# Hybrid layers on one core: the attention mask written by ScalarE, VectorE's rotary step moved between subtraction and row sums

## What is computed

```
x = x + linear_attention(layernorm(x))
x = x + ffn(layernorm(x))
x = x + retention(layernorm(x))
x = x + ffn(layernorm(x))
```

```
q, k = l2norm(q) * qs, l2norm(k) * ks           # then rotary tables with a scale
sim  = q k^T * 8, over this block of 32 keys and the one before
sim  = where(key after query, or more than 32 before it, or no such block, -max, sim)
x    = softmax(sim) v Wo + x
x    = (a * gelu(gate)) W2 + b2 + x             # a, gate = layernorm(shift(x)) W1 + b1
```

## Time and profile before

| what | value |
|---|---|
| median of three runs | 3166.11 us |
| profiled execution, its own time | 3168.24 us |
| its span | 3166.5 us |
| busy share: TensorE, VectorE, ScalarE, GpSimd | 95%, 91%, 72%, 57% |
| mean granted clock of TensorE | 0.99 of full |

### The profile page before, as it was taken

How to read it: one execution, slowest core, us unless ns; L and a number is a source line. 1 busy time by engine, 2 the same in 40 slices (tenths; PEclk the granted TensorE clock), 3 DMA queues, 4 the chain that set the end, 5 groups by cost and what they waited for, 6 DMA issues and landing times.

```text
span 3166.5 us, 93664 instructions
## 1 busy us (share of the span) xinstructions
PE 3005.7 (95%) x37896; PEld 1857.5 (59%) x37896; DVE 2880.3 (91%) x2671; ACT 2272.7 (72%) x3707; POOL 1807.9 (57%) x823
## 2 busy tenths in 40 slices
PE   8699999999999999999999999999999999999996
PEld 4356555665665566565566656556656555665653
DVE  5599999999999999999999999999999999999995
ACT  4467777777777777776667777777777777777774
POOL 8556565555656555555445565555656565555652
PEclk9799999999999999999999999999999999999998
DMA  9544544543544544454344354454445445445542
GB/s 317 169 110 116 144 115 107 145 122 98 156 117 101 144 117 117 118 154 113 84 133 106 91 152 117 107 133 124 112 121 141 112 122 133 112 118 134 125 112 59
DMA packets 254405, 398.04 MB, mean 126 GB/s; under 512 B 51148, under 2 KB 84872, under 8 KB 254280
## 3 DMA queue, kind: packets, MB, share of 16 engines
q1 hardware_dynamic: 254280, 396.41, 47.8%
HBM read 64.64 MB, written 19.92 MB: 27 GB/s over the span
## 4 chain that ended last, share of the span: by engine, by line
PE 40%; DVE 23%; ACT 19%; issue 10%; SPq 1%; POOL 1%; DMA 1%; DVEq 0%; ACTq 0%; POOLq 0%
PE ps L848 6%; PE ps L806 5%; PE ps L866 5%; PE ps L882 5%; PE ps L827 5%; PE ps L787 4%; ACT f_ab L1094 4%; DVE f_mx L1362 4%; DVE f_p L1365 3%; ACT f_u L1093 3%; DVE f_p L1377 3%; ACT ps L1105 3%; PE ps L789 3%; PE ps L788 3%; ACT f_p L1111 3%
## 5 line engine op out<-in xcount | busy, mean ns | idle before, releaser
L1291 POOL TENSOR_TENSOR f_w<-f_w,f_ab 128x1024 f32<-128x1024 f32 x192 | 549.2, 2861 | 526.9 <-DVE f_w L1342 526.9
L1296 POOL TENSOR_TENSOR f_ab<-f_w,f_rn 128x1024 f32<-128x1024 f32 x192 | 594.1, 3094 | 390.9 <-DVE f_rn L1352 380.9
L1287 POOL TENSOR_TENSOR f_u<-f_u 128x512 f32<-128x512 f32 x384 | 589.1, 1549 | 365.3 <-ACT f_u L1093 359.8
L1094 ACT ACTIVATE f_ab<-ps,f_pa 128x512 f32<-128x512 f32 x768 | 542.1, 706 | 1.2
L1093 ACT ACTIVATE f_u<-ps 128x512 f32<-128x512 f32 x768 | 467.1, 608 | 99.3 <-PE ps L789 93.6
L1342 DVE TENSOR_TENSOR f_w<-f_ab,f_tan 128x1024 f32<-128x1024 f32 x384 | 500.4, 1343 | 4.1 <-POOL f_ab L1296 2.3
L848 PEld LDWEIGHTS ps<-f_tb,f_v 128*64 128x64 f32 x6144 | 396.0, 137 | 102.1 <-issue 78.5
L848 PE MATMUL ps<-f_tb,f_v 128*64 128x160 f32 (+1 forms) x6144 | 442.2, 297 | 11.9 <-DMA f_tb<-f_pt 10.7
L1105 ACT ACTIVATE ps<-ps 128x512 f32<-128x512 f32 x384 | 204.7, 574 | 340.7 <-PE ps L806 340.2
L787 PE MATMUL ps<-f_xh,f_wh 128*128 128x512 f32 x768 | 380.7, 496 | 54.8 <-ACT f_ab L1094 44.5
L806 PE MATMUL ps<-f_u,f_ones 128*128 128x512 f32 x768 | 370.2, 604 | 6.9 <-POOL f_u L1287 4.1
(11 more groups left out here) (165 smaller groups left out, 4822.9 us busy)
## 6 DMA issues: line engine op xcount, KB each, us to landing
f_kb<-f_ab SPq DMA_DIRECT2D x384, 256.0 KB, 3.6
f_qb<-f_ab SPq DMA_DIRECT2D x384, 256.0 KB, 3.6
f_tb<-f_pt SPq DMA_DIRECT2D x1344, 64.0 KB
f_wh<-split_w SPq DMA_DIRECT2D x48, 384.0 KB, 4.4
f_wl<-split_w SPq DMA_DIRECT2D x48, 384.0 KB, 4.2
a_w_raw<-wqkv SPq DMA_DIRECT2D x24, 384.0 KB, 4.6
split_w<-a_w_hi SPq DMA_DIRECT2D x24, 384.0 KB, 4.6
split_w<-a_w_lo SPq DMA_DIRECT2D x24, 384.0 KB, 5.5
```

Source lines behind the costliest of these rows:

```text
L1094: nc.scalar.activation(ab[:, g % 2, i, :], bank("qk", g, i), ACT.Identity, scale=pa[:, g, i:i + 1]).then_inc(qk_read.sem, 1)
L1287: nc.gpsimd.tensor_tensor(u[:, 2 * i + 1, :], u[:, 2 * i, :], u[:, 2 * i + 1, :], ALU.add).then_inc(sq_sum[i].sem, 1)
L1291: nc.gpsimd.tensor_tensor(w[:, 0:2, :], w[:, 0:2, :], ab[:, k % 2, 0:2, :], ALU.add).then_inc(q_sum.sem, 1)
L1296: nc.gpsimd.tensor_tensor(ab[:, k % 2, 0:2, :], w[:, 0:2, :], rn[:, 0:1, :].broadcast_to([128, 2, N]), ALU.mult).then_inc(rope_q.sem, 1)
```

## The change

- ScalarE gets a function `mask_scores(g)`: one copy of the table, read twice, into both banks 5 and 6 (128 partitions x 1024 elements). It waits for the subtraction of the quad before. It stands in ScalarE's order after `evacuate_out(-3)` (quad -1), before `inverse_norms(1)` (quad 0), before `shifted` (quad 1) and after `next_high` (quad 2); in retention steps quad 2's stands after `gates`.
- TensorE loses both mask matmuls and the identity that they used. `scores(g)` waits for ScalarE's copy and increments a semaphore that nobody waits for. At the start of the kernel two matmuls write both banks once.
- In plain steps, `scores(0)` goes in front of the last of the four banks of `project(2)`.
- In plain steps, VectorE does `turn(1)` between `less_maximum(-1)` and `sums(-1)`, and `turn(2)` between `less_maximum(0)` and `sums(0)`; before, `turn(1)` stood after `sums(-1)`, and `turn(2)` after `residual`. Retention steps had this place for `turn(2)` already.
- Step 0 gets a wait in `norms`.

The diff, with most of the unchanged lines left out:

```diff
@@ -464,6 +464,7 @@
         s_ready = per_quad("s_ready", ahead=2)
+        m_ready = per_quad("m_ready")
         s_max, s_sub, p_exp = per_quad("s_max"), per_quad("s_sub", ahead=1), per_quad("p_exp")
@@ -480,6 +481,7 @@
         R.update(g0=Signal("r_g0"), g1=Signal("r_g1", 2), g2=Signal("r_g2"))
+        scores_begun = sem("scores_begun")
         r_consts, r_turned, stored = sem("r_consts"), sem("r_turned"), sem("stored")
@@ -489,7 +491,7 @@
                     *((128, c) for c in range(-64, 33, 32)), *((512, c) for c in range(-640, -255, 128))]
-        ACT_USES = [(1, -1), (3, -5), (3, -4), (3, -3), *((4, c) for c in range(-3, 2)), *((8, c) for c in range(-7, 1)),
+        ACT_USES = [(1, -1), (3, -5), (3, -4), (3, -3), *((4, c) for c in range(-4, 2)), *((8, c) for c in range(-7, 1)),
                     *((16, c) for c in range(-15, 1)), (32, 32), *((128, c) for c in range(-96, 1, 32))]
@@ -507,7 +509,6 @@
                 mask, ones = t("mask", [128, 768], BF16), t("ones", [128, 128])
-                identb = t("identb", [128, 128], BF16)
                 xs, xh, x1 = t("xs", [C, N]), t("xh", [C, N], F32R), t("x1", [C, N])
@@ -533,7 +534,7 @@
                 split_first = sem("f_split_first", scope)
-                N_CONST, N_MASKED = 6 * 16, 3
+                N_CONST, N_MASKED = 6 * 16, 2
                 block = scope.enter_context(nc.Block())
@@ -799,6 +800,9 @@
+        if not prev and g:
+            pe.wait_ge(gain.sem, now.count(gain, g - 1))
         for i in range(2):
@@ -806,15 +810,12 @@
-    def mask_scores(g):
-
-        pe.wait_ge(s_sub.sem, now.count(s_sub, g - 1))
-        nc.tensor.matmul(ps[:, SS[0], :], identb[:, :], mask[:, 128:640], start=True, stop=False, skip_group_check=True)
-
...
         pe.wait_ge(k_dma.sem, now.count(k_dma, g))
-        nc.tensor.matmul(ps[:, SS[1], :], identb[:, :], mask[:, 128:640], start=True, stop=False, skip_group_check=True)
+        pe.wait_ge(m_ready.sem, now.count(m_ready, g))
+        pe.sem_inc(scores_begun, 1)
         for tile in range(TILES):
@@ -952,7 +953,6 @@
         project(0, (0, 1))
-        mask_scores(-1)
         project(0, (2, 3))
@@ -966,7 +966,6 @@
         project(1, (2, 3))
-        mask_scores(0)
         project_out(0)
@@ -983,7 +982,6 @@
         mean()
-        mask_scores(1)
         project(3, (0, 1))
@@ -992,7 +990,6 @@
         ret_values()
-        mask_scores(2)
         ret_project("q")
@@ -1003,8 +1000,6 @@
-    if prev:
-        mask_scores(-1)
     if cur:
@@ -1012,6 +1007,9 @@
             pe.wait_ge(masked, N_MASKED)
+            for i in range(2):
+                nc.tensor.matmul(ps[:, SS[i], :], ones[:, :], tan2[:, 0, :], start=True, stop=True).then_inc(masked, 1)
     if prev:
@@ -1029,15 +1027,13 @@
         norms(1)
-        mask_scores(0)
-        project(2, range(4))
+        project(2, range(3))
         scores(0)
+        project(2, (3,))
         project_v(1, range(2))
...
         values(-1)
-    if cur:
-        mask_scores(1)
     if prev:
@@ -1106,6 +1101,13 @@
+    def mask_scores(g):
+        act.wait_ge(s_sub.sem, now.count(s_sub, g - 1))
+        if not prev and g == 0:
+            act.wait_ge(masked, N_MASKED + 2)
+        nc.scalar.activation(ps[:, SS[0]:SS[1] + 1, :], mask[:, 128:640].unsqueeze(1).broadcast_to([128, 2, N]), ACT.Copy).then_inc(m_ready.sem, 1)
@@ -1187,6 +1189,7 @@
         evacuate_out(-3)
+        mask_scores(-1)
         inverse_norms(0)
@@ -1199,12 +1202,14 @@
         ret_square2()
+        mask_scores(0)
         inverse_norms(1)
...
         evacuate_out(-1)
+        mask_scores(1)
         shifted()
@@ -1218,6 +1223,7 @@
         gates()
+        mask_scores(2)
         evacuate_out(0, (0,))
@@ -1524,21 +1534,21 @@
         less_maximum(-1)
+    if cur:
+        turn(1)
+    if prev:
         sums(-1)
-    if cur:
-        turn(1)
-    if prev:
         turn_weights(-1)
...
         less_maximum(0)
+        turn(2)
         sums(0)
...
     if cur:
-        turn(2)
         add_keys(2)
@@ -1578,7 +1588,6 @@
                     nc.vector.tensor_copy(mask[:, :].rearrange("p (a n) -> p a n", a=2), hid[:, 0:2, 0:384]).then_inc(masked, 1)
-                    nc.vector.tensor_copy(identb[:, :], fc[:, 0:128]).then_inc(masked, 1)
                     nc.vector.tensor_copy(ones[:, :], fc[:, 128:256]).then_inc(masked, 1)
```

More of the change, by code:

```diff
@@ L1526, in step @@
                             less_maximum(-1)
-                            sums(-1)
                         if cur:
@@ L1530, in step @@
                         if prev:
+                            sums(-1)
                             turn_weights(-1)
```

## The result

| what | before | after |
|---|---|---|
| median of the runs | 3165.95 us (4 runs) | 3468.38 us (4 runs, 3467.27 to 3471.75) |
| ratio, 95% interval | | 1.0957 (1.0938 to 1.0976) |
| profiled execution, its own time | 3168.24 us | 3467.27 us |
| its span | 3166.5 us | 3465.5 us |
| mean granted clock of TensorE | 0.99 | 0.95 |

What follows compares the result with a forecast made beforehand. A step was taken as VectorE's stretch up to `residual`, ScalarE's run and a short tail. 42 x (4.9 + 0.5) = 227, + 15 = 242 us more gave 3408 us (from the profiled 3410), range 3270 to 3485.

Steps and rivals of the forecast that it cites:

- mask in the tail: Quad 2's mask copy behind `next_high` delays the scores: 0.5 us in 42 plain steps, plus 15 us for retention steps.
- rival (a): TensorE's clock falls in its gap before `mean`: 1.7 us in each of 42 steps, 3480 us; chance 0.15.
- +4.9 us a step: Plain steps: `turn(2)` waits for GpSimd, then port conflicts; `residual` ends at 829.85 instead of 824.95, bounds 3.1 to 5.5.
- It isn't added: `turn(1)` among GpSimd's square sums makes `turn_weights(-1)` 1 us late; the wait of `turn(2)` takes it up, so nothing added.
- GpSimd's 821.93: End of `normalise_queries(1)` in the traced plain step, which `turn(2)` must await; kept unchanged in the forecast.
- ScalarE's run: Gapless 17.2 us from `shifted` to `next_high`, starting when `residual` ends; forecast to stay as long as before.
- Rival (b): VectorE alone is the bound and 2.3 us leaving the second half come back: 42 x 2.6 = 109, 3275 us; chance 0.13.
- +0.5 us a step: Quad 2's 1.0 us mask copy behind `next_high` delays `scores(2)`, less VectorE's slack; bounds 0 and 1.05.
- Against it: at 57 us of work in a step the engine stays mostly busy: Argument that TensorE's clock would hold despite standing some 4 us in each step before `mean`.
- +3 us in each: Five retention steps: `mask_scores(2)` comes after ScalarE's table load, 2.9 us late for everything behind; +15 us, bounds 0 and 20.
- TensorE waits for the others in the chain above, so I cost this gain at nothing: Mask matmuls leaving TensorE, 148 us of busy time, some 2.3 us a step, counted as zero gain.
- the masks in ScalarE's waits: Mask copies for quads -1, 0 and 1 precede instructions ScalarE already waits for, so cost nothing; otherwise 1 us each.

Runs made afterwards that it cites:

- two_w: The changed kernel with the query half of `w` doubled, so turn(k) waits for normalise_queries(k - 2), for timing only: 3438.68 us, ratio 1.0861.
- gpsimd_order: The changed kernel with GpSimd doing queries 1 and normalise 1 ahead of quad 2's squares in plain steps: 3408.51 us, ratio 1.0765.
- turn1_back: The changed kernel with turn(1) alone put back behind sums(-1): 3450.38 us, ratio 1.0895.
- turns_back: The changed kernel with both turns put back, masks on ScalarE and the place of scores(0) still changed: 3212.88 us, ratio 1.0152.
- quad2_mask_on_pe: turns_back with the mask of quad 2 alone written by TensorE again, as two matmuls: 3151.69 us, ratio 0.9951.
- fill: The changed kernel with norms(2) done three times in plain steps, to fill TensorE's gap before the mean: 3440.05 us, ratio 1.0868.
- masks_only: quad2_mask_on_pe with scores(0) also back behind all four banks of quad 2: 3151.02 us, ratio 0.9963.
- split_order: quad2_mask_on_pe with exponential and row sums of quads 3 and 0 in halves, and GpSimd's queries 1 ahead of squares 2: 3110.12 us, ratio 0.9805.

## Why the prediction came out as it did

The sign, the mechanism and the place were right; the size was 60 us short. By the experiments' own differences the account is: rotation 258 (forecast 42 x 4.9 = 206), mask in the tail 61 (forecast 42 x 0.5 + 15 = 36), three masks off TensorE -15 (forecast 0). That is 304 of the measured 302, against 242. The plain steps, 68.2 us for the most part, miss the 66 to 67 that the prediction gave as the sign of being right, and the granted clock fell, its sign of rival (a).

**The rotation, "+4.9 us a step".** From the keys' normalisation of quad 3 to the end of `residual` VectorE takes 5.2 us more than before (43.2 for 38.0). The parts: the wait of `turn(2)` for line 1338's buffer 3.60 (forecast 3.3), the pair 2.36 (2.34), the weights' product held by the port to 2.08 us (2.1). Of the 0.3 us by which the wait is longer, half is the start, 0.13 us after line 1306's end; the other half isn't explained.

That VectorE would find the port taken, and wholly, not by half, is what the rows of `turn(1)`, two_w and gpsimd_order show: 4.44, 5.50 and 4.39 us for a pair of 2.34. Taken one by one, the four instructions around `turn(1)` end at 802.00 (GpSimd), 803.08 (VectorE), 804.24 (GpSimd) and 805.32 (VectorE), each its own 1.1 to 1.2 us after the one before; sharing would have let both engines' pairs end close together. This is the exclusive lock of the Trainium skill (SBUF — State Buffer, "Who interferes with whom").

**`turn(1)`, 4.4 us, "It isn't added".** The duration is right, 4.44. That the wait of `turn(2)` would take its lateness up is right only in part: turn1_back won 18 us. `turn(1)` makes VectorE 0.6 us later at the wait, but it makes the end of the wait 0.6 us later as well, since VectorE's shifted work now holds GpSimd's second square sum of quad 2 (1.97 us for 1.38). The step took GpSimd's 821.93 for fixed; a lock works both ways.

**ScalarE's run.** It starts with `residual` and is closed by the logarithms, as the forecast had it, and `residual` being late makes the step late: ScalarE's wait before `shifted` was forecast at 5 us or more and is 5.92. Rival (b), by which the slack behind `residual` would come back, is refuted: the plain intervals are 6.5 us longer, not 2.6, although VectorE has 2.35 us without work before `centred`'s 1405.

**"+0.5 us a step" for the mask of quad 2.** The nearest row for the copy was 1008 ns, and it is 1048:

```profile
L1109 ACT ACTIVATE ps<-f_mask 128x1024 f32<-128x1024 bf16 x192 | 201.2, 1048 | 0.1
```

The term was still under-sized: turns_back against quad2_mask_on_pe gives 0.87. Some 0.25 us from the end of the copy to the first score (845.35 to 845.60) were left out, since the working compared the end of one ScalarE instruction with the start of the other. The 0.5 us of slack that VectorE had was right: the run and its tail are 1.9 us longer, the step's second half 1.4.

**Rival (a), the clock.** It was given 0.15 and 1.7 us a step, as an alternative. It happened together with the forecast, at less than half its price: the gap before the mean is 4.78 us (4 was said), the clock falls to 0.50 in every plain step, and by fill that is worth 0.6 us a step on average, 0.8 in the usual one. The part that counts is what ScalarE waits for while TensorE is slow, 0.41 us at 833.34 and the slower scores; its run, 17.2 us before, is 17.7 now. The statement in the Trainium skill (TensorE: Matmul & The Clock Gate, Part 1) that an idle TensorE falls to 1.2 GHz holds here, also for an engine that is 87% busy. The step that failed is "Against it: at 57 us of work in a step the engine stays mostly busy": a mean share over the step was put against one gap inside it. The trace of the kernel before had a nearer row than the earlier trace rows, a gap of 4.19 us, with 6.8 us at 0.50 from just before its end (TensorE; then window, length, busy us of PE, PEld, DVE, ACT, POOL, granted clock, DMA share, GB/s):

```profile
152.09 0.61 PE L817 MATMUL ps<-f_mask,f_identb 128*128 128x512 bf16 x1 [4.19 <-DMA f_qb<-f_ab]
...
151.40:158.20 6.80, 6.11 (x138) 4.73 (x138) 6.73 (x6) 4.03 (x8) 5.50 (x2) 0.50 0.34 77
```

**Retention steps, "+3 us in each".** It is 5.3. The 2.9 us were the distance from the scores' start to the end of the table load; the wait is 3.32 us, the mask's own 1.03 us between them included. What the forecast didn't have is the clock behind that wait: scores and value half together take 2.6 us longer at 0.50.

**"TensorE waits for the others in the chain above, so I cost this gain at nothing".** The three masks that went brought 15 us (masks_only). What was missed, as far as the trace shows it, is a way around: TensorE's norms earlier, hence GpSimd's square sum, hence a VectorE instruction that is held by the port for less. That the place of `scores(0)` changes nothing, and that the masks in ScalarE's waits are free, came out as said.

Sum for the usual plain step, from the measured parts: 5.2 (rotation) + 0.87 (mask) + 0.8 (clock) - 0.35 (three masks) = 6.5 us, against 6.8 in the trace. Each part comes from another pair of kernels; 0.3 us stays without a name.

## What to carry to other kernels

Before an instruction is moved forward to fill a wait, look at what it needs itself: here a 1.12 us wait was filled with work that could not start for 3.6 us, because the other engine's order had been written for the old place. Moving that engine's order along (gpsimd_order) took the wait away and still won only 60 of the 302 us, since the two engines then met at the port; what made the kernel faster than before, by 61 us, was to leave the instruction where it was, give three masks to ScalarE's idle time, split the work that was waited for, and change GpSimd's order to suit VectorE's (split_order). Where two engines share a port, a wait removed on one comes back as a longer duration beside it, so look at durations that are above their usual value and at what ends just before they do. And look at an engine's longest gap in the step, not at its busy share alone, when asking whether its clock will hold.

## What the runs showed of the hardware that was not expected

- VectorE's instructions with two SBUF inputs and GpSimd's alternate when both have more to do: a pair of 2.34 us takes 4.4 to 5.5 us with GpSimd instructions between, and GpSimd's 2.35 us become 3.2 to 3.4. VectorE's subtraction, which reads the scores from PSUM, keeps its 1.2 us beside a busy GpSimd (814.04, beside GpSimd's 813.96).
- In the changed kernel TensorE, after one gap of 4.78 us in a step of 68 us, works at 0.50 of its clock for 3.4 or 6.8 us. In fill, with `norms(2)` done three times over in front of it (5.31 us in place of 1.88), the gap is 0.90 us and the clock stays at 1.00 there.
- ScalarE's copy of 128x1024 from bf16 in SBUF to two PSUM banks is 1048 ns, and the first matmul that waited for it starts about 0.25 us after its end.
